# Attention in a mixture-of-experts block on one core: causal masks moved behind the exponential, and two small jobs moved to ScalarE and GpSimd

## The reference

```python
c_q = x @ W_dq;  Q = (c_q @ W_uq).reshape(B, S, 16, 16)
c_kv = x @ W_dkv
K = (c_kv @ W_uk).reshape(B, S, 16, 16);  V = (c_kv @ W_uv).reshape(B, S, 16, 16)
scores = einsum('bqhd,bkhd->bhqk', Q, K) / math.sqrt(16)
scores = where(tril(ones((S, S))), scores, -inf)
out = einsum('bhqk,bkhd->bqhd', softmax(scores, axis=-1), V).reshape(B, S, 256) @ W_o
```

## Time and profile before

| | |
|---|---|
| median of 3 runs | 1255.91 us (1251.33 to 1259.59) |
| profiled execution | span 1263.3 us; no other time of it was kept |
| attention | about 423 to 920 us of the span |
| PE / DVE / ACT / POOL busy, whole span | 84% / 66% / 53% / 30% |
| one step in the middle of the attention | 30.7 us |

### The profile page before, as it was taken

The page is one execution under the profiler, slowest core; times in us unless marked ns, Lnnn a source line. Parts: engine busy times, 40 slices in busy tenths (PEclk is TensorE's granted clock), DMA queues, the critical chain, the costliest instruction groups (busy, mean ns, idle before and its releaser), DMA issues. The chain is left out here.

```text
span 1263.3 us, 22520 instructions
## 1 busy us (share of the span) xinstructions
PE 1066.7 (84%) x6988; PEld 642.3 (51%) x6988; DVE 829.9 (66%) x2536; ACT 666.1 (53%) x1668; POOL 384.3 (30%) x404
## 2 busy tenths in 40 slices
PE   3539999984988899999999999999859369999940
PEld 2328888872442244443444444444347258888840
DVE  6774444436867888888888888888037754444427
ACT  5605554542753376676777666667636315455520
POOL 6506777752002000000000000000048227777730
PEclk8559999995977699999999999999889759999985
DMA  9503333326756444444444444440057113333339
GB/s 301 186 9 93 101 105 105 102 84 216 201 200 142 59 60 61 61 61 60 61 61 60 60 61 61 61 60 11 10 189 239 58 38 94 104 102 104 105 118 331
DMA packets 109248, 132.53 MB, mean 105 GB/s; under 512 B 29968, under 2 KB 83664, under 8 KB 109136
## 3 DMA queue, kind: packets, MB, share of 16 engines
q1 hardware_dynamic: 91280, 89.65, 31.2%
q0 software_dynamic: 13632, 37.24, 9.3%
q10 hardware_dynamic: 4224, 4.19, 1.0%
HBM read 82.42 MB, written 48.23 MB: 103 GB/s over the span
## 5 line engine op out<-in xcount | busy, mean ns | idle before, releaser
L1415 ACT ACTIVATE stacks_rows_or_prob<-stacks_bank 128x512 f32<-128x512 f32 (+3 forms) x768 | 326.0, 494 | 144.1 <-PE stacks_bank L1347 118.9
L1429 DVE CUSTOM_DVE_ANT_0 stacks_bank<-stacks_bank,all_causal 128x128 f32<-128x128 f32 (+3 forms) x512 | 245.4, 504 | 33.7 <-PE stacks_bank L1318 30.2
L1432 DVE TENSOR_REDUCE t_maxp<-stacks_bank 128x1 f32<-128x512 f32 x256 | 175.5, 686 | 25.0 <-PE stacks_bank L1318 24.4
L1318 PE MATMUL stacks_bank<-stacks_kst,stacks_qst 96*128 96x512 bf16 (+2 forms) x528 | 160.3, 348 | 8.5 <-DVE t_maxp L1429 4.2
L1358 PE MATMUL stacks_bank<-stacks_rows_or_prob,stacks_turned_or_values 128*32 128x512 f32 (+3 forms) x1536 | 164.5, 500 | 3.0 <-ACT stacks_rows_or_prob L1415 1.1
L1344 PE MATMUL stacks_bank<-stacks_qst,stacks_kst 99*128 99x512 bf16 (+3 forms) x528 | 154.9, 335 | 2.5 <-ACT stacks_rows_or_prob L1415 1.9
L1296 POOL COPY stacks_turned_or_values<-stacks_values 128x512 f32<-128x512 f32 x16 | 9.8, 613 | 427.7 <-DMA stacks_kst<-qk_parts 286.5
L1318 PEld LDWEIGHTS stacks_bank<-stacks_kst,stacks_qst 96*128 96x128 bf16 x528 | 48.5, 98 | 126.9 <-DVE t_maxp L1429 66.6
L653 PE MATMUL be_psG<-b_w,be_xT 128*128 x426 | 112.8, 401 | 0.0
L653 PE MATMUL ae_psG<-a_w,ae_xT 128*128 x426 | 111.9, 398 | 0.0
L1347 PE MATMUL stacks_bank<-all_causal_t,all_ident_bf 128*128 128x128 bf16 x512 | 109.6, 221 | 0.0
(11 more groups left out here) (296 smaller groups left out, 1917.7 us busy)
## 6 DMA issues: line engine op xcount, KB each, us to landing
stacks_qst<-qk_parts SPq DMA_DIRECT2D x66, 128.0 KB, 4.9
stacks_kst<-qk_parts SPq DMA_DIRECT2D x66, 128.0 KB, 7.6
stacks_rows_or_prob<-y_rows SPq DMA_DIRECT2D x16, 512.0 KB, 6.1
s_yk<-y_rows SPq DMA_DIRECT2D x16, 512.0 KB, 9.4
stacks_parts_or_stacks<-qk_parts SPq DMA_DIRECT2D x60, 128.0 KB, 6.2
qk_parts<-stacks_parts_or_stacks SPq DMA_DIRECT2D x16, 384.0 KB, 2.6
qk_parts<-q_parts SPq DMA_DIRECT2D x16, 384.0 KB, 3.4
o_rows<-t_orow SPq DMA_DIRECT2D x32, 136.0 KB, 8.7
```

The lines of the kernel that those rows point to most:

```text
L1318: nc.tensor.matmul(psR[bank][:, 0:w], qst[slot][0:KROWS, h, i * P:(i + 1) * P], kst[slot][0:KROWS, h, k0:k0 + w], start=True, stop=True).t ...
L1415: nc.scalar.activation(prob[j % 2][:, h, a:(c + 1) * 512], psS[n % ST_BANKS][:, a - c * 512:512], ACT.Exp, scale=DK ** -0.5).then_inc(exp_ ...
L1429: ins = nc.vector.tensor_tensor_reduce(psR[bank][:, 0:w], psR[bank][:, 0:w], T.causal[:, 512 - w:512], 1.0, -BIG, ALU.add, ALU.max, maxp[: ...
L1432: ins = nc.vector.tensor_reduce(maxp[:, h, col:col + 1], psR[bank][:, 0:w], AX_X, ALU.max)
```

## The change

The table of -1e30 is no longer added in the transposed scores. The four diagonal blocks of a block row j, one for each head and 128 by 128, get a unit of their own that fills one bank: `(j, c, None, 512)`, four matmuls. ScalarE reads it twice: `Relu` with scale -1/4 into an SBUF tile `below`, then, one unit later, `Exp` with scale -1 from `below` into `prob`. The clamp keeps the masked part from overflowing. GpSimd then sets the part above the diagonal to 0 (`mask`, an affine select over 4 x 128 columns), and the `pv` of that block waits for it. The other pieces shrink to what is right of the diagonal, and those of width 0 go.

`copy_rows` moves from VectorE to ScalarE. The three-way split of the maxima moves from VectorE to GpSimd (`split_max`); VectorE keeps only the negation. GpSimd's copy of the values moves two steps ahead of its use. The planner has new costs and runs over the new units.

```diff
+def transposed_units():
+    units = []
+    for j in range(QT):
+        for c in range(j // QHALF, 2):
+            if c == j // QHALF:
+                units.append((j, c, None, HG * P))
+            w = (c + 1) * 512 - max(c * 512, (j + 1) * P)
+            units += [(j, c, h, w) for h in range(HG) if w > 0]
+    return units
...
-            t = start + (w + P * (max(c * 512, j * P) == j * P)) / 2.4
-            act = max(act, t + READER_LATENCY) + 100 + w * 0.833
+            t = start + w / 2.4
+            act = max(act, t + READER_LATENCY) + 70 + w * 0.833
             st_free[n_st % ST_BANKS] = act + 60
             exp_end[j, c, h] = act + 100
+            if h is None:
+                act += 110 + w * 0.833
+                exp_end[j, c, h] = act + MASK_LATENCY
...
+        def split_max(g):
+            pool.wait_ge(drained, drained_to(max_at[g]))
+            wait(pool, m_loaded, g * (16 * PARTS))
+            nc.gpsimd.tensor_copy(mparts[:, 0], neg[:]).then_inc(split, 1)
+            pool.wait_ge(split, g * SPLIT + 1)
+            nc.gpsimd.tensor_tensor(mid[:], neg[:], mparts[:, 0], ALU.subtract).then_inc(split, 1)
+            pool.wait_ge(split, g * SPLIT + 2)
+            nc.gpsimd.tensor_copy(mparts[:, 1], mid[:]).then_inc(split, 1)
+            pool.wait_ge(split, g * SPLIT + 3)
+            nc.gpsimd.tensor_tensor(mparts[:, 2], mid[:], mparts[:, 1], ALU.subtract).then_inc(m_ready, 1)
+
+        def mask(g, j):
+            pool.wait_ge(diagonal, g * QT + j + 1)
+            block = prob[j % 2][:, :, j * P:(j + 1) * P]
+            nc.gpsimd.affine_select(out=block, in_=block, compare_op=ALU.is_ge, fill=0.0, base=0,
+                                    pattern=[[0, HG], [1, P]], channel_multiplier=-1).then_inc(masked, 1)
+
+        def step(g, k, later, with_before):
+            order = plans[later, with_before][0]
+            done = [x[1] for x in order[:order.index(("m", 1))] if x[0] == "pv"] if later else []
+            split_behind = max(done, default=-1)
+            for j in range(QT):
+                mask(g, j)
+                if later and j == max(split_behind, 0):
+                    split_max(g + 1)
+            if later > 1:
+                values_of(g + 2, (k + 2) % SLOTS)
...
-            if a == j * P:
-                ins = nc.tensor.matmul(ps[:, 0:P], T.ident_bf[:], T.causal_t[:], start=False, stop=True)
+            if h is None:
+                for x in range(HG):
+                    ins = nc.tensor.matmul(ps[:, x * P:(x + 1) * P], kst[k][0:MROWS, x, keys], qst[k][0:MROWS, x, keys],
+                                           start=True, stop=True)
...
-            pe.wait_ge(exp_done, g * ST + n_st[j, c, HG - 1] + 1)
+            pe.wait_ge(st_read, g * ST + n_st[parts_of(st_units, j, c)[-1]] + 1)
+            if j // QHALF == c:
+                pe.wait_ge(masked, g * QT + j + 1)
...
+        def exp_diagonal(g, j, n):
+            act.wait_ge(st_read, g * ST + n + 1)
+            nc.scalar.activation(prob[j % 2][:, :, j * P:(j + 1) * P], below[:, j % 2].rearrange("p (h t) -> p h t", h=HG), ACT.Exp,
+                                 scale=-1.0).then_inc(diagonal, 1)
+
+        def copy_rows(g, c):
+            r = out_at(g, c) - 1
+            act.wait_ge(filled, r + 1)
+            wait(act, o_stored[c], g * 16)
+            nc.scalar.copy(orow[:, c], psR[r % RING_BANKS][:].rearrange("p (x w) -> p x w", w=VW)[:, :, 0:OW]).then_inc(rows_copied, 1)
...
-            wait(dve, m_loaded, g * (16 * PARTS))
+            wait(dve, m_ready, g)
             nc.vector.tensor_scalar(neg[:], psR[bank][0:MROW, 0:P], -1.0, None, ALU.mult).then_inc(drained, 1)
-            dve.wait_ge(drained, r + 1)
-            link(nc.vector.tensor_copy(mparts[:, 0], neg[:]), g, 2)
-            link(nc.vector.tensor_tensor(mid[:], neg[:], mparts[:, 0], ALU.subtract), g, 3)
-            link(nc.vector.tensor_copy(mparts[:, 1], mid[:]), g, 4)
-            nc.vector.tensor_tensor(mparts[:, 2], mid[:], mparts[:, 1], ALU.subtract).then_inc(m_ready, 1)
```

More of the change, by code:

```diff
@@ L1118, in score_units, with parts_of @@
     return units
+def transposed_units():
[7 more added lines that the diff above has]
+    return units
+def parts_of(units, j, c):
+    return [unit[:3] for unit in units if unit[:2] == (j, c)]
 def plan_step(units, later, with_before):
     width = lambda j, c: min((c + 1) * 512, S) - max(c * 512, j * P)
+    st = transposed_units()
     ring = [("s", u, 1) for u in range(AHEAD, len(units))] if later else []
@@ L1213, in programs_attention @@
     o_stored = [M.sem(f"o_stored{c}") for c in range(2)]
-    m_loaded, filled, drained, max_ready, m_ready, st_done, exp_done, pv_done, o_copied, pool_done, chain = (
-        M.sem(n) for n in ("m_loaded", "filled", "drained", "max_ready", "m_ready", "st_done", "exp_done", "pv_done",
-                           "o_copied", "pool_done", "chain"))
+    m_loaded, filled, drained, rows_copied, max_ready, m_ready, st_done, st_read, diagonal, masked, pv_done, o_copied, \
+        pool_done, joined, split = (
+            M.sem(n) for n in ("m_loaded", "filled", "drained", "rows_copied", "max_ready", "m_ready", "st_done", "st_read", "diagonal",
+                               "masked", "pv_done", "o_copied", "pool_done", "joined", "split"))
     RING0 = NS + 1 + AHEAD
@@ L1224, in programs_attention, with drained_to, free_bank @@
     assert RING % RING_BANKS == 0 and ST % ST_BANKS == 0
+    kinds = ["s"] * NS + ["m"] + ["s"] * AHEAD
+    for g in range(NG):
+        kinds += [x[0] for x in plans[min(2, NG - 1 - g), g > 0][1]]
+    kinds += ["o"] * 2
+    max_at = [r for r, kind in enumerate(kinds) if kind == "m"]
+    copied_by_act = list(itertools.accumulate(kind == "o" for kind in kinds))
+    def drained_to(r):
+        return r + 1 - copied_by_act[r]
+    def free_bank(pe, r):
+        before = r - RING_BANKS
+        if before >= 0 and kinds[before] == "o":
+            pe.wait_ge(rows_copied, copied_by_act[before])
+        elif before >= 0:
+            pe.wait_ge(drained, drained_to(before))
     def steps(step):
@@ L1312, in gpsimd @@
         pool.wait_ge(Q.v_ready, Q.CH)
+        values_of(0, 0)
+        for s in range(1, SLOTS):
+            blank(s)
+        pool.wait_ge(Q.v_ready, 2 * Q.CH)
+        for stored in Q.parts_stored:
+            pool.wait_ge(stored, (Q.CH // 2) * (16 * Q.NU))
+        first.link(nc.gpsimd.memset(kst[SLOTS - 1][KROWS:MROWS, :, :], 1.0))
+        split_max(0)
+        values_of(1, 1)
         steps(step)(pool)
@@ L1328, in turn_max @@
         def turn_max(g, r, bank):
[L1329 removed]
+            free_bank(pe, r)
             pe.wait_ge(max_ready, g + 1)
@@ new lines, in copy_rows @@
+        def copy_rows(g, c):
[3 more added lines that the diff above has]
+            nc.scalar.copy(orow[:, c], psR[r % RING_BANKS][:].rearrange("p (x w) -> p x w", w=VW)[:, :, 0:OW]).then_inc(rows_copied, 1)
+        def step(g, k, later, with_before):
+            order = plans[later, with_before][0]
+            turned = [sum(x[0] == "st" for x in order[:order.index(("o", c))]) if with_before else None for c in range(2)]
+            for n, (j, c, h, w) in enumerate(st_units):
+                if n == n_st[parts_of(st_units, j, c)[0]]:
+                    if j > 1:
+                        act.wait_ge(pv_done, g * PV + n_pv[j - 2, c] + 1)
+                    else:
+                        wait(act, pv_done, (g - 1) * PV + n_pv[j + QHALF * (c + 1) - 2, c] + 1)
+                act.wait_ge(st_done, g * ST + n + 1)
+                if h is None:
+                    nc.scalar.activation(below[:, j % 2], psS[n % ST_BANKS][:], ACT.Relu, scale=-(DK ** -0.5)).then_inc(st_read, 1)
+                else:
+                    nc.scalar.activation(prob[j % 2][:, h, (c + 1) * 512 - w:(c + 1) * 512], psS[n % ST_BANKS][:, 0:w], ACT.Exp,
+                                         scale=DK ** -0.5).then_inc(st_read, 1)
+                if n and st_units[n - 1][2] is None:
+                    exp_diagonal(g, st_units[n - 1][0], n - 1)
+                for half in range(2):
+                    if n == turned[half]:
+                        copy_rows(g - 1, half)
+                if (j, c) == (QHALF + 1, 1) and st_units[n + 1][0] > j:
@@ L1422, in scalar @@
         steps(step)(act)
+        for c in range(2):
+            copy_rows(NG - 1, c)
     def row_max(dve, u, r, bank):
```

84 lines of the change are left out of this document (30 added, 54 removed).

## The result

The changed kernel takes 1300.5 us (median of 4 runs, 1297.3 to 1302.4) against 1254.1 for the kernel before on the same chip: ratio 1.034, 95% interval 1.030 to 1.039. The forecast was 1284, range 1241 to 1303. Its profiled execution has a span of 1300.1 us.

A forecast was written before the change was run, and what follows sets the result against it. The prediction took PE as the bound. Fifteen steps at +0.6 us (+9), the last step (+3) and the start (+0.6) made +13 us at full clock; the clock's +15 made +28, so 1284 us, range 1241 to 1303.

The forecast's parts named there:

- forecast, clock held: One attention step at full clock: -1.0 up to the turn, +1.5 new wait, +0.1 afterwards, +0.6 us in sum.
- The new wait: PE at block row 5's `pv` waits for GpSimd's mask, queued behind the split: +1.5 us a step (+0.8 to +2.8).
- rival price for the split: Split on GpSimd by the skill's factor 1.96: 2.0 us, making the sum 0.5 us a step, 7 us in all, higher.
- From the `pv` to the end of the step: From block row 5's `pv`, eight masks gone but a longer chain to the last `pv`: +0.1 us a step.
- Up to the turn: PE's list ahead of the turn of the maxima loses 23 of 32 masks: -1.0 us a step (-1.4 to -0.5).
- The mask's price: Each mask matmul on PE costs the distance of two starts, 0.06 us; 32 make 1.9 us a step.
- The added work: ScalarE goes from 19.7 to 24.3 us a step, stays under 30, so is not the bound over a step.
- The clock: PE's still stretch lowers its clock in about half to two thirds of the steps, 1.7 us each: +15 us.
- the last step and the start: Last step, without ring units, alternates between PE and ScalarE: +3 us; split at the attention's start on GpSimd: +0.6 us.
- Clock stays up: Rival: PE's stall is there but its clock does not fall: +5 to +18, about 1268 us; chance 0.26.
- GpSimd fast enough, the saving stands: Rival: split and mask quick enough for block row 5's `pv`, PE's saving stands: -13 to -27, about 1238 us; chance 0.18.
- ScalarE becomes the bound: Rival: ring units wait for ScalarE's row copies, 1 us each step: +15 on the first case, 1299 us; chance 0.08.

The follow-up runs named there:

- C: The changed kernel plus 18 unused 256-column matmuls on PE between the turn of the maxima and the waiting `pv`: 1276.8 us, ratio 1.015.
- A: The changed kernel with GpSimd's split of the maxima placed behind the mask of block row 5 instead of ahead of it: 1260.4 us, ratio 1.001.
- F: The kernel before without its 32 mask matmuls a step, exponentials touching the diagonal at scale 0.01 (output not the reference's): 1245.4 us, ratio 0.994.
- H: The kernel before plus eight unused 512-column ScalarE passes a step, one behind each diagonal block row: 1263.8 us, ratio 1.007.
- N: The kernel before with VectorE's plain maxima reading half their columns, all exponentials at scale 0.01 (output not the reference's): 1247.4 us, ratio 0.993.
- E: A with ScalarE reading the diagonal bank once: no `Relu`, one `Exp` from PSUM at scale 0.01 (diagonal probabilities changed): 1252.3 us, ratio 0.998.
- B: The changed kernel with the split of the maxima back on VectorE: 1258.9 us, ratio 1.000.
- M: F with VectorE's plain maxima reading half their columns, all exponentials at scale 0.01 (output not the reference's): 1234.1 us, ratio 0.982.

## Why the prediction was right, and where it was right for less than its reasons

The three terms of a step, read from PE's starts: from the turn to the `pv` of block row 5, from there to the next step's first instruction, and on to the next turn (usual values; the change's second and third are those of the step shown above):

| | turn to `pv` | `pv` to next step | next step to turn | step |
|---|---|---|---|---|
| before | 1.57 | 4.23 | 24.92 | 30.72 |
| forecast, clock held | +1.5 | +0.1 | -1.0 | +0.6 |
| C (clock held) | 3.40, +1.83 | 4.34, +0.11 | 24.67, -0.25 | +1.69 |
| the change | 3.39 | 5.09 | 24.98 | 33.46 |
| A | 0.70 | 5.14 | 24.92 | 30.76 |
| F | 1.54 | 4.15 | 24.32 | 30.01 |

**The new wait: right, a little small.** The working had 0.95 to the end of the negation, 1.5 split, 0.6 mask, 0.1 hand-overs, 3.1 in all; the trace has 0.97, 0.07 to the first cast, 1.62 for the split (two casts of 0.28, two subtractions of 0.42, and gaps), about 0.6 for the mask and 0.13 more: 3.39. PE stood still 2.62 us, forecast 2.7. The term was forecast at +1.5 us a step and is +1.83 in C. The rule of the Trainium skill (GPSIMD Engine Reference, Performance versus the Vector engine) gave the rival price for the split: 2.0 us as an estimate, by its factor of 1.96. The trace has 1.62, between that and my 1.5 and nearer to mine; on VectorE the split took 1.0.

**From the `pv` to the end of the step, +0.1: right.** C has +0.11. In the change this stretch is 5.09 us, since most of it ran at the lower clock.

**Up to the turn, -1.0: the step that failed.** It is -0.25 in C and nothing in A and in the change. Two errors stand in it. *The mask's price.* I took the distance of two starts, 0.06 us, for what goes when the instruction goes. F, which removes the masks and nothing else, gives 0.71 a step for what I counted as 1.9, and 0.60 ahead of the turn for what I counted as 1.3. From a step's start to its turn in F:

```profile
597.19 0.39 PE L1318 MATMUL stacks_bank<-stacks_kst,stacks_qst 96*128 96x512 bf16 x1
...
621.51 0.27 PE L1331 MATMUL stacks_bank<-all_ident,t_maxq 128*32 128x128 f32 x1
```

The waits of F, longer than before, speak for this reading: the matmuls behind a removed mask start earlier only until they meet a bank that VectorE or ScalarE has not read. I had dismissed those waits as mostly hidden behind a running matmul and taken "busy 29.2 of 29.5 us" for "no room". H and N refute that: PE is busier in H, where the step is longer, and the step shortens in N, where only VectorE is relieved. *The added work.* I counted 4.6 us a step more for ScalarE at nothing since it stays under the step; E and H show +0.27 and +0.44. ScalarE also took more than estimated, 82 to 84 of 100 us in A, 25.7 us a step for 24.3.

**The clock, +15 us: right in the total, by two errors that cancel.** I chose a fall in 0.6 of the steps, at 1.7 us; it fell in 12 of 13. The 15 steps of the change are 16.4 us longer than C's, 1.4 us for each fall: 1.05 in the usual step (33.46 - 32.41) and 3 in the two longest (35.5). That the total came out is luck.

**The sum.** Forecast: +9 for the steps at full clock, +15 for the clock, +4 for the last step and the start, 28. In the traces the 15 steps at full clock are +22 (C less before), and the clock +16. The last step, from the last negation to the last copy of rows, is 1.9 us longer (36.4 for 34.5) where I had 3. That makes 41; the medians have 46, with a 95% interval of 38 to 48. So of what the forecast lacked, most is the saving that did not come (0.75 us a step, 11 us) and the rest the wait (0.3 us a step, 5 us). With these two put right it would have been 1300; as it stands, 1300 is at the upper end of the range.

**The rivals.** *Clock stays up* (1268): falls by the windows; C, which has that clock, is at 1277 and not at 1268, since the saving is missing there too. *GpSimd fast enough, the saving stands* (1238): false twice; even with the `pv` 0.70 us behind the turn and hardly any wait for GpSimd (B) the step is 30.92 and does not break even. Its break-even point, 2.5 us behind the turn, assumed the saving of 1.0. *ScalarE becomes the bound* (1299): the measured time is close to it, but not by its mechanism: A has all of ScalarE's work and is at 1260; E shows 0.27 us a step of it.

**What stays open.** Of the 1.9 us of mask time, 0.7 comes back as time and relieving VectorE's plain maxima gives 0.43 more (M less F), of which 0.27 come with the masks in place too (N). The rest was not settled: the waits point to the masked maxima and, once those ease, to ScalarE's banks, but no run cut the masked maxima, or both engines at once. Nor was it settled which part of the change makes the 0.48 us from F to E.

## What to carry to other kernels

Before work moves to an idle engine, read what will be queued behind it there and who waits for that: the split cost 0.08 us a step on an idle GpSimd and 40 us in all with a mask behind it that PE waits for. Where three engines pass banks to each other in order, the price of a removed instruction is not its own time; take away one kind of instruction and measure, since a busy share of 98% covers small waits. And a still stretch of PE in every step can be paid twice, once for itself (25 us here) and once for the clock (16 us); the stretches of 0.66 us in C were paid once.
